# Edge sums of a graph layer: products as the stationary operand, one-hots of 64 nodes as the moving one

## The chip, the core and the metric

The kernel runs on one core of a Trainium2 chip. The metric is the device time of one execution in microseconds. Before the change three runs took 1311.8, 1334.03 and 1337.46 us, a median of 1334.03 us. TensorE is called PE, its weight loads PEld, VectorE DVE, ScalarE ACT, GpSimd POOL, and the queue of SyncE SP.

## The reference, cut to what matters

A graph layer on 3125 nodes and 50000 edges (sorted by destination) is followed by a mixture of experts. The graph layer, with constants left out:

```python
h0, h1 = x0 @ W_lin1_0 * z, einsum('nuc,uv->nvc', x1, W_lin1_1) * z      # node table h, 256 numbers a node
hid = silu(edge_length_embedded @ fc_w0)                                # 8 -> 64 an edge ("radial")
wA, wB, wC, wD = split(hid @ fc_w1)                                     # 4 x 64 an edge
xs0, xs1 = h0[edge_src], h1[edge_src]                                   # the gather
midA = wA * xs0 * sh0
midD = wD * einsum('euc,ec->eu', xs1, sh1) / sqrt(3)
midB = (wB * xs0)[:, :, None] * sh1[:, None, :]
midC = wC[:, :, None] * xs1 * sh0[:, None, :]
y = segment_sum(concat(midA, midD, midB, midC), edge_dst)               # the edge sums
out = s + (y @ W_lin2) * z                                              # then a residual and a layer norm
```

Everything is float32. A second layer norm, a router, a shared expert and eight routed experts (two a token) follow.

## The kernel before

The program is a chain of blocks, each with its own instruction streams for the five engines and a barrier at its end: `node_block`, `edge_block`, `update_block`, and the expert blocks. Nothing schedules the work: the order on each engine is the order in the text, and semaphores that count steps tie the engines together.

`node_block` (from line 134) normalises 25 tiles of 128 nodes and writes the table `h_tab` to memory. POOL clears `y_sb` (L262) and splits the edge lengths `ele` into a rounded high part and a remainder (L265, L267), which SP writes out as `ele_split`; it splits the two radial weight matrices too (L270 to L275). The high and low parts stand in a reduced type (F32R): a product of such operands takes one pass of PE per column, and two terms restore the precision.

`edge_block` (from line 448) works in T = 98 steps of 512 edges, four groups (C = 4) of 128 edges each. One more loop, over rounds r, repeats all steps when the destinations of some step span more nodes than the window; here one round is enough (392 gathers are 98 x 4), and since the widest step spans 37 nodes, a window of 64 nodes needs one round as well. In each step:

- SP loads the edge lengths of the step (L518); PE multiplies them with `w0` (`hidden`, L720, one matmul of 512 columns); ACT applies the silu (L566).
- DVE rounds the result (`high`, L616) and takes the remainder (`low`, L621); PE multiplies with `w1hi` and `w1lo` (`radial`, L728 and L729, eight matmuls of 256 columns, contraction over 128 rows).
- POOL copies the step's source numbers and factors sh to small tiles (L543, L547) and issues four gathers of 128 rows (L552) into one of two buffers `rows`.
- DVE compares the destinations with 0 to 127 (`one_hot`, L607, 512 elements a partition); ACT scales each one-hot with the four sh of its edge (`scale_hot`, L576, 16 instructions of 128 columns).
- DVE forms eight products of 64 a group (`products`, L634 and L636, one pair a group).
- PE sums over edges (`segment`): the scaled one-hots [128 edges x 128 nodes] are stationary, the products move. Each group is one matmul of 256 columns (L740) and three of 128 (L743), in plain float32.
- DVE adds the result, 128 nodes by 512, to `y_sb` in two halves of 64 partitions (`add_y`, L651).

PE runs in each turn `hidden(t+2)`, `radial(t+1)`, `segment(t)`; DVE runs `add_y(t-1)`, `high(t+2)`, `one_hot(t+2)`, `low(t+2)`, `products(t+1)`. In the trace one plain float32 matmul is two weight loads and two matmul records, one F32R matmul is one of each.

`update_block` (from line 764) takes 25 tiles: POOL copies 128 nodes of sums (L879), PE transposes them (`turn`, L1057, four matmuls), ACT copies the result (L983), PE multiplies with W_lin2 (`mix`, L1067, four float32 matmuls with 64 moving columns). Then come residual, norm, transposes and router scores (L1078, L1086 with 8 stationary columns, L1098).

## Time and profile before

| | us |
|---|---|
| median of 3 runs | 1334.03 |
| the profiled execution: its span | 1334.0 |
| node block | 0 to 65.5 |
| edge block, from the barrier to the first edge sum | 65.5 to 78.4 |
| edge block, first edge sum to the last | 78.4 to 682.2 |
| end of the edge block, update block | 682.2 to 779 |
| experts | 779 to 1334.0 |

The profiled execution's own time is the span of 1334.0 us; it is also the median run, so nothing lies between the two. Start times in the rows are microseconds from the start of the span. In rows of a timeline, instructions that are alike and follow each other are merged (x8), and the duration runs from the start of the first to the end of the last; a matmul's end is modelled, so paces are read from starts. An engine's idle time before a row stands in brackets, with what ended it.

### The profile page before, as it was taken

The page shows a single profiled execution, that of the slowest core. Times are in us where ns is not written, and L with a number is a line of the kernel's source. Part 1 is how long each engine was busy: PE and PEld are TensorE (multiplying, and loading weights), DVE is VectorE, ACT ScalarE, POOL GpSimd, SP SyncE. Part 2 cuts the span into 40 slices and gives each one's busy share as a digit, 9 for nine tenths or more (in the row PEclk, how much of TensorE's full clock was granted, in tenths as well). Part 3 has the DMA queues.
Part 4 walks back from the last instruction along what each step waited for, and adds up shares of the span by engine and source line. Part 5 has one row for each costly group of instructions (what it writes and reads, how often), then busy time and mean ns, then how long its engine had stood idle before and what let it go on. Part 6 is the DMA issues. An engine that isn't in the chain of part 4 may idle for free. (4 is left out here: it accounts for less than half of the span.)

```text
span 1334.0 us, 32063 instructions
## 1 busy us (share of the span) xinstructions
PE 1217.9 (91%) x8631; PEld 1120.6 (84%) x8632; DVE 1029.3 (77%) x2584; ACT 826.6 (62%) x2362; POOL 720.3 (54%) x823
## 2 busy tenths in 40 slices
PE   2789999999999999999989899998998997989995
PEld 2578888888888888888887679998998997989995
DVE  7589999999999999999856866444765674666663
ACT  2688888888888888888834674453442443343431
POOL 7178888788887888878731104651242232233332
PEclk9989999999999999999975979999999998999998
DMA  6443444344344444434543474764324334332232
GB/s 241 155 131 111 120 117 119 111 119 120 111 122 120 115 116 118 121 110 118 171 126 116 163 259 131 251 216 140 99 44 103 78 62 99 95 95 46 46 49 28
DMA packets 107219, 160.47 MB, mean 120 GB/s; under 512 B 16414, under 2 KB 82750, under 8 KB 106656
## 3 DMA queue, kind: packets, MB, share of 16 engines
q1 hardware_dynamic: 73680, 90.86, 21.4%
q0 software_dynamic: 29568, 65.62, 20.6%
q10 hardware_dynamic: 3920, 3.41, 0.8%
q8 instruction: 19, 0.31, 0.1%
q14 instruction: 32, 0.26, 0.1%
HBM read 110.99 MB, written 48.85 MB: 120 GB/s over the span
## 5 line engine op out<-in xcount | busy, mean ns | idle before, releaser
L576 ACT ACTIVATE hots<-hot,sh_st 128x128 f32<-128x128 f32 x1568 | 467.9, 390 | 3.8 <-PE psY L743 3.3
L552 POOL DMA_INDIRECT rows<-h_tab,src_st x392 | 404.9, 1033 | 117.2 <-issue 116.9
L743 PEld LDWEIGHTS psY<-prod,hots 128*128 128x128 f32 x2352 | 324.6, 192 | 20.4
L743 PE MATMUL psY<-prod,hots 128*128 128x128 f32 x2352 | 326.1, 275 | 0.0
L1739 POOL DMA_INDIRECT out_rows<-q_ob,q_index x58 | 125.5, 2163 | 294.4 <-DVE q_ob L1837 193.3
L740 PE MATMUL psY<-prod,hots 128*128 128x256 f32 x784 | 234.4, 381 | 0.6 <-DVE prod L636 0.6
L636 DVE TENSOR_TENSOR prod<-psW,rows 128x384 f32<-128x384 f32 x392 | 213.8, 545 | 0.0
L1763 ACT ACTIVATE q_hf<-q_psA,q_b 128x256 f32<-128x256 f32 x232 | 109.7, 473 | 111.7 <-PE q_psA L1293 109.0
L1300 PE MATMUL q_psB<-x_whi,q_hhi 128*128 128x256 f32 x464 | 138.7, 299 | 24.5 <-DVE q_hlo L1815 24.5
L651 DVE TENSOR_TENSOR y_sb<-y_sb,psY 64x512 f32 x196 | 133.4, 681 | 10.2 <-issue 5.7
L1293 PE MATMUL q_psA<-q_xhi,x_whi 128*128 128x256 f32 x464 | 133.2, 287 | 4.0 <-DVE q_xlo L1804 2.8
L1300 PE MATMUL q_psB<-x_wlo,q_hhi 128*128 128x256 f32 x464 | 133.7, 288 | 0.0
L1300 PE MATMUL q_psB<-x_whi,q_hlo 128*128 128x256 f32 x464 | 133.7, 288 | 0.0
L1293 PE MATMUL q_psA<-q_xlo,x_whi 128*128 128x256 f32 x464 | 131.5, 283 | 0.0
L1293 PE MATMUL q_psA<-q_xhi,x_wlo 128*128 128x256 f32 x464 | 131.5, 283 | 0.0
L728 PE MATMUL psW<-w1hi,cols_hi 128*128 128x256 f32 x392 | 108.2, 309 | 16.2 <-DVE cols_hi L621 6.5
L740 PEld LDWEIGHTS psY<-prod,hots 128*128 128x128 f32 x784 | 119.4, 191 | 0.8 <-DVE prod L636 0.8
L634 DVE TENSOR_TENSOR prod<-psW,rows 128x128 f32<-128x128 f32 x392 | 110.5, 282 | 5.4 <-DMA rows<-h_tab,src_st 1.8
L1300 PEld LDWEIGHTS q_psB<-x_whi,q_hhi 128*128 128x128 f32 x464 | 90.6, 195 | 28.0 <-issue 27.0
L566 ACT ACTIVATE hid<-psE 128x512 f32<-128x512 f32 x98 | 58.7, 598 | 89.2 <-PE psE L720 87.6
L728 PEld LDWEIGHTS psW<-w1hi,cols_hi 128*128 128x128 f32 x392 | 75.0, 191 | 45.8 <-issue 45.1
L729 PE MATMUL psW<-w1lo,cols_hi 128*128 128x256 f32 x392 | 98.0, 283 | 0.0
(213 smaller groups left out, 2509.6 us busy)
## 6 DMA issues: line engine op xcount, KB each, us to landing
x_raw<-in_w SPq DMA_DIRECT2D x18, 1024.0 KB, 8.0
slots_d<-blank SPq DMA_DIRECT2D x49, 258.0 KB
x_slot_tile<-slots_d SPq DMA_DIRECT2D x30, 258.0 KB, 2.8
s_row<-xn_d SPq DMA_DIRECT2D x50, 128.0 KB, 3.1
cols_lo<-ele_split SPq DMA_DIRECT2D x196, 32.0 KB
rows<-h_tab,src_st POOLq DMA_INDIRECT x392, 2.8
x_sb<-in_x SPq DMA_DIRECT2D x5, 640.0 KB, 5.8
h_tab<-x_sb ACTq DMA_DIRECT2D x5, 640.0 KB, 3.3
```

What stands on the lines that cost most here:

```text
L552: pool.indirect_dma_start(out=rows[p][:, c, :, :].rearrange("p a u -> p (a u)"), out_offset=None, in_=h_tab, in_offset=bass.IndirectOffset ...
L576: ins = nc.scalar.activation(hots[p][:, 4 * c + k, :], hot[p][:, c, :], ACT.Copy, scale=sh_st[p][:, 4 * c + k:4 * c + k + 1])
L634: nc.vector.tensor_tensor(slots[:, 0::7, :], w[:, 0:2, :], rows[p][:, c, 0:1, :].to_broadcast([P, 2, MUL]), ALU.mult)
L636: nc.vector.tensor_tensor(slots[:, 1:7, :].rearrange("p (b k) u -> p b k u", b=2), w[:, 2:4, :].unsqueeze(2).to_broadcast([P, 2, 3, MUL]), ...
L651: ins = nc.vector.tensor_tensor(acc, acc, psY[p][lo:lo + HALF, :], ALU.add)
L728: nc.tensor.matmul(o, hidT[p][:, P * c:P * c + P], w1hi[:], start=True, stop=False)
L740: ins = nc.tensor.matmul(y[:, 1::2, :], hots[p][:, 4 * c, :], a[:, 4:8, :], start=(c == 0), stop=(c == C - 1), skip_group_check=True)
L743: ins = nc.tensor.matmul(y[:, 2 * k::6 - 2 * k, :][:, 0:2, :], hots[p][:, 4 * c + k + 1, :], a[:, 0::k + 1, :][:, 0:2, :], start=False, st ...
L1293: ins = nc.tensor.matmul(ps, w1_part(w, k, f), x(k), start=(n == 0), stop=(n == len(terms) - 1))
L1300: ins = nc.tensor.matmul(ps, h, w2_part(w, f), start=(f == 0 and n == 0), stop=(f == FC - 1 and n == 2))
L1739: pool.indirect_dma_start(out=out, out_offset=bass.IndirectOffsetOnAxis(ap=index[m][:], axis=0), in_=ob[m][:], in_offset=None, compute_op= ...
L1763: nc.scalar.activation(hf[f][:], psA[f % 4][:, 0:TOK], ACT.Gelu, bias=b1_st[:, f:f + 1]).then_inc(gelu_done, 1)
```

## The change

- `segment` is transposed. The products are stationary, two blocks of 64 at a time (128 columns), and the scaled one-hots of a window of SPAN = 64 nodes move. There are five matmuls a group: two with the sh0 one-hot, on products (0,1) and (2,3), then one for each of the three sh1 one-hots, on products (4,5), (5,6) and (7,8). `products` writes nine blocks of 64 instead of eight, in four instructions a step instead of eight. The sums stand transposed in `yT` [128, 5, 3264], and `add_y` adds one tile of 128 by 320.
- The radial network runs in plain float32: `hidden` has a contraction of 16 rows and 256 columns (the two halves of the step stand beside each other in the block-diagonal `w0`), and `radial` has four matmuls of 64 rows and 256 columns, in the order of groups 0, 2, 1, 3; groups 0 and 1 use rows 0 to 63, groups 2 and 3 rows 64 to 127. `high`, `low`, `ele_split` and all splitting on POOL go.
- Silu, `one_hot` and `scale_hot` work on 256, 256 and 64 elements instead of 512, 512 and 128.
- POOL's copies go. The gathers are unrolled over 98 steps with a ring of seven buffers (four of them in memory borrowed from `wlo0`), one semaphore a buffer; SP loads sh for each step.
- In `update_block` the transposes and both copies go; `mix` is five float32 matmuls of 128 moving columns on a zero-padded `w2`, which ten small loads fill.

```diff
+SPAN = 64
+REG = 5
+NCOL = NPAD + SPAN
...
-            y_sb = gkeep("y_sb", [P, NT + 1, 8, MUL])
+            yT = gkeep("yT", [P, REG, NCOL])
...
-                residue = ekeep("residue", [P, T, C])
...
+                w0 = ekeep("w0", [2 * NB, P])
+                fc_w = ekeep("fc_w", [P, 4, MUL])
...
-            sp.dma_start(e_raw, ele_t.rearrange("b e -> (b e)").rearrange("(p w) -> p w", p=P)).then_inc(e_in, 16)
-            for dst, src in ((src_sb, v["src_t"]), (dst_ti, v["dst_t"]), (sh_sb, v["sh_t"])):
+            for dst, src in ((src_sb, v["src_t"]), (dst_ti, v["dst_t"])):
                 sp.dma_start(dst[:].rearrange("p t c -> p (t c)"), src).then_inc(tab_in, 16)
+            for n, column in enumerate((1, 0, 3, 2)):
+                sp.dma_start(fc_w[:, n, :], v["fc1"][:, MUL * column:MUL * (column + 1)]).then_inc(fc_in, 16)
             sp.wait_ge(fczero, 1)
             sp.wait_ge(pool_step, 2)
             for half in range(2):
-                sp.dma_start(w0raw[32 * half:32 * half + 2 * NB, :], v["fc0"]).then_inc(fc_in, 16)
-            sp.dma_start(w1raw[:], v["fc1"]).then_inc(fc_in, 16)
+                sp.dma_start(w0[NB * half:NB * (half + 1), MUL * half:MUL * (half + 1)], v["fc0"][0:NB, 0:MUL]
+                             ).then_inc(fc_in, 16)
...
-            flat = ele_split.rearrange("r e -> (r e)").rearrange("(h p w) -> h p w", h=2, p=P)
-            sp.wait_ge(e_split_hi, 1)
-            sp.dma_start(flat[0], e_hi.bitcast(F32)).then_inc(e_out, 16)
...
-            link(pool.memset(y_sb[:], 0.0))
...
+            link(pool.memset(yT[:], 0.0))
...
+    PART = STEP // 2
+    RING = 7
+    USES = T // RING
+    TURN = 2 * RING
+    assert T % TURN == 0
...
-        rows = [sb(f"rows{i}", [P, C, 4, MUL]) for i in range(2)]
-        prod = [sb(f"prod{i}", [P, C, 8 * MUL]) for i in range(2)]
-        hot = [sb(f"hot{i}", [P, C, P]) for i in range(2)]
-        hots = [sb(f"hots{i}", [P, 4 * C, P]) for i in range(2)]
+        hid = [sb(f"hid{i}", [P, PART]) for i in range(2)]
+        LENT = WW // (C * FEAT)
+        rows = [v["wlo0"][:, C * FEAT * i:C * FEAT * (i + 1)].bitcast(F32).rearrange("p (c a u) -> p c a u", c=C, a=4)
+                for i in range(LENT)]
+        rows += [sb(f"rows{i}", [P, C, 4, MUL])[:] for i in range(RING - LENT)]
+        prod = [sb(f"prod{i}", [P, C, 9, MUL]) for i in range(2)]
+        hot = [sb(f"hot{i}", [P, C, SPAN]) for i in range(2)]
+        hots = [sb(f"hots{i}", [P, C, 4, SPAN]) for i in range(2)]
...
-                            sp.dma_start(e_st[p][32 * half:32 * half + 2 * NB, :].bitcast(F32),
-                                         ele_split[:, at(first_edge, STEP)]).then_inc(e_in[p], 16)
+                            sp.dma_start(e_st[p][NB * half:NB * (half + 1), :],
+                                         ele_t[:, at(first_edge + PART * half, PART)]).then_inc(e_in[p], 16)
+                        first_sh = sp.snap(t * (4 * C))
+                        sp.wait_ge(hots_done, r * T + t + 1)
+                        sp.dma_start(sh_st[p][:], sh_t[:, at(first_sh, 4 * C)]).then_inc(sh_in[p], 16)
...
             with pool.Fori(0, R) as r:
-                with pool.Fori(0, T // 2) as k:
...
+                for t in range(T):
+                    pool.wait_ge(prod_done, (r * T + t) * 2 + 2)
+                    pool.sem_inc(gather_turn, 1)
+                    for c in range(C):
+                        pool.indirect_dma_start(
+                            out=rows[t % RING][:, c, :, :].rearrange("p a u -> p (a u)"), out_offset=None, in_=h_tab,
+                            in_offset=bass.IndirectOffsetOnAxis(ap=src_sb[:, t, c:c + 1], axis=0),
+                        ).then_inc(row_in[t % RING], 16)
...
-                act.wait_ge(low_done, r * T + j + 1)
-                nc.scalar.activation(hid[p][:], psE[:], ACT.Silu, scale=1.0 / float(np.sqrt(NB))).then_inc(silu_done, 1)
-            def scale_hot(r, j, p):
-                act.wait_ge(sh_staged, r * T + j + 1)
+                act.wait_ge(w_done, r * T + j + 1)
+                nc.scalar.activation(hid[p][:], psE[p][:, 0:PART], ACT.Silu,
+                                     scale=1.0 / float(np.sqrt(NB))).then_inc(silu_done, 1)
+            def scale_hot(r, k, j, p):
+                act.wait_ge(sh_in[p], 16 * (r * (T // 2) + k + 1))
                 act.wait_ge(hot_done, r * T + j + 1)
                 act.wait_ge(seg_done, r * T + j + 1)
                 for c in range(C):
-                    for k in range(4):
-                        ins = nc.scalar.activation(hots[p][:, 4 * c + k, :], hot[p][:, c, :], ACT.Copy,
-                                                   scale=sh_st[p][:, 4 * c + k:4 * c + k + 1])
+                    for n in range(4):
+                        ins = nc.scalar.activation(hots[p][:, c, n, :], hot[p][:, c, :], ACT.Copy,
+                                                   scale=sh_st[p][:, 4 * c + n:4 * c + n + 1])
...
-                nc.vector.tensor_tensor(hot[p][:], iota_row[:].unsqueeze(1).to_broadcast([P, C, P]),
-                                        key[:, at(j), :].rearrange("p o c -> p (o c)").unsqueeze(2).to_broadcast([P, C, P]),
+                nc.vector.tensor_tensor(hot[p][:], iota_row[:, 0:SPAN].unsqueeze(1).to_broadcast([P, C, SPAN]),
+                                        key[:, at(j), :].rearrange("p o c -> p (o c)").unsqueeze(2).to_broadcast([P, C, SPAN]),
                                         ALU.is_equal).then_inc(hot_done, 1)
...
-            def high(r, j, p):
...
+            def products(r, turn, j, p, ring):
                 dve.wait_ge(w_done, r * T + j + 1 + 2)
                 dve.wait_ge(seg_done, r * T + j + 1)
-                for c in range(C):
...
+                dve.wait_ge(row_in[ring], 16 * C * (r * USES + turn + 1))
+                w, x, out_p = psW[p], rows[ring], prod[p]
+                nc.vector.tensor_tensor(out_p[:, :, 1:4, :], w[:, :, 2:3, :].to_broadcast([P, C, 3, MUL]),
+                                        x[:, :, 1:4, :], ALU.mult)
+                nc.vector.tensor_tensor(out_p[:, :, 0, :], w[:, :, 0, :], x[:, :, 0, :], ALU.mult).then_inc(prod_done, 1)
+                nc.vector.tensor_tensor(out_p[:, :, 4::2, :], w[:, :, 3:4, :].to_broadcast([P, C, 3, MUL]),
+                                        x[:, :, 1:4, :], ALU.mult)
+                nc.vector.tensor_tensor(out_p[:, :, 5::2, :], w[:, :, 1:2, :].to_broadcast([P, C, 2, MUL]),
+                                        x[:, :, 0:1, :].to_broadcast([P, C, 2, MUL]), ALU.mult).then_inc(prod_done, 1)
             def add_y(r, j, p):
-                low_tile = dve.value_load(low_row[0:1, at(j)], min_val=0, max_val=NT)
-                high_tile = dve.value_load(high_row[0:1, at(j)], min_val=0, max_val=NT)
+                low = dve.value_load(low_row[0:1, at(j)], min_val=0, max_val=NPAD)
                 dve.wait_ge(seg_done, r * T + j + 1 + 2)
                 dve.wait_ge(y_done, r * T + j + 2)
-                for lo, tile in ((0, low_tile), (HALF, high_tile)):
-                    acc = y_sb[lo:lo + HALF, at(tile), :, :].rearrange("p o a u -> p (o a u)")
-                    ins = nc.vector.tensor_tensor(acc, acc, psY[p][lo:lo + HALF, :], ALU.add)
-                ins.then_inc(y_done, 1)
+                acc = yT[:, :, at(low, SPAN)]
+                nc.vector.tensor_tensor(acc, acc, psY[p][:, 0:REG * SPAN].rearrange("p (g n) -> p g n", g=REG), ALU.add
+                                        ).then_inc(y_done, 1)
...
+                def turn_of(r, k, q, last=False):
+                    j = k * TURN + 2 + q
+                    add_y(r, j - 2, q % 2)
+                    if not last:
+                        one_hot(r, j + 1, (q + 1) % 2)
+                    products(r, k * 2 + (2 + q) // RING, j, q % 2, (2 + q) % RING)
+                with dve.Fori(0, T // TURN - 1) as k:
+                    for q in range(TURN):
+                        turn_of(r, k, q)
...
-                nc.tensor.matmul(psE[:], w0[:], e_st[p], start=True, stop=True).then_inc(hid_done, 1)
+                nc.tensor.matmul(psE[p][:, 0:PART], w0[:], e_st[p][:], start=True, stop=True
+                                 ).then_inc(hid_done, 1)
             def radial(r, j, p):
-                pe.wait_ge(low_done, r * T + j + 1 + 2)
-                pe.wait_ge(prod_done, (r * T + j) * C + C)
-                for c in range(C):
-                    o = psW[p][c // 2][:, 256 * (c % 2):256 * (c % 2) + 256]
-                    nc.tensor.matmul(o, hidT[p][:, P * c:P * c + P], w1hi[:], start=True, stop=False)
-                    ins = nc.tensor.matmul(o, hidT[p][:, P * c:P * c + P], w1lo[:], start=False, stop=True)
+                pe.wait_ge(silu_done, r * T + j + 1 + 2)
+                pe.wait_ge(prod_done, (r * T + j) * 2 + 2 * RING - 2)
+                for c in (0, 2, 1, 3):
+                    part = slice(MUL * (c // 2), MUL * (c // 2) + MUL)
+                    ins = nc.tensor.matmul(psW[p][:, c, :, :],
+                                           hid[p][part, P * (c % 2):P * (c % 2) + P],
+                                           fc_w[part, :, :], start=True, stop=True)
                 ins.then_inc(w_done, 1)
             def segment(r, j, p):
                 pe.wait_ge(hots_done, r * T + j + 1 + 2)
                 pe.wait_ge(y_done, r * T + j + 1)
-                y = psY[p][:, :].rearrange("p (a u) -> p a u", u=MUL)
+                y = psY[p][:, 0:REG * SPAN].rearrange("p (g n) -> p g n", g=REG)
+                pe.wait_ge(prod_done, (r * T + j) * 2 + 1 + 2 * RING)
                 for c in range(C):
-                    pe.wait_ge(prod_done, (r * T + j) * C + c + 1 + 2 * C)
-                    a = prod[p][:, c, :].rearrange("p (a u) -> p a u", u=MUL)
-                    ins = nc.tensor.matmul(y[:, 1::2, :], hots[p][:, 4 * c, :], a[:, 4:8, :], start=(c == 0),
-                                           stop=(c == C - 1), skip_group_check=True)
-                    for k in range(3):
-                        ins = nc.tensor.matmul(y[:, 2 * k::6 - 2 * k, :][:, 0:2, :], hots[p][:, 4 * c + k + 1, :],
-                                               a[:, 0::k + 1, :][:, 0:2, :], start=False, stop=(c == C - 1),
+                    for g in range(2):
+                        nc.tensor.matmul(y[:, g, :], prod[p][:, c, 2 * g:2 * g + 2, :].rearrange("p a u -> p (a u)"),
+                                         hots[p][:, c, 0, :], start=(c == 0 and g == 0), stop=(c == C - 1),
+                                         skip_group_check=True)
+                pe.wait_ge(prod_done, (r * T + j) * 2 + 2 + 2 * RING)
+                for c in range(C):
+                    for n, first in enumerate((4, 5, 7)):
+                        ins = nc.tensor.matmul(y[:, 2 + n, :],
+                                               prod[p][:, c, first:first + 2, :].rearrange("p a u -> p (a u)"),
+                                               hots[p][:, c, n + 1, :], start=False, stop=(c == C - 1),
...
+            top, bottom = slice(0, MUL), slice(MUL, P)
+            w_a, w_d = v["w_20"][0:MUL, :], v["w_20"][MUL:2 * MUL, :]
+            w_b, w_c = v["w_21"][0:MUL, :], v["w_21"][MUL:2 * MUL, :]
+            sp.wait_ge(wzero, 1)
+            for part, g, n, block_w in ((top, 0, 0, w_a), (bottom, 0, 1, w_c), (top, 1, 0, w_c), (bottom, 1, 1, w_c),
+                                        (top, 2, 0, w_d), (bottom, 2, 1, w_b), (top, 3, 1, w_b), (bottom, 3, 0, w_d),
+                                        (top, 4, 1, w_b), (bottom, 4, 0, w_d)):
+                sp.dma_start(w2[part, g, n, :], block_w).then_inc(w_in, 16)
             sp.dma_start(wr[:], v["w_r"].rearrange("(k p) e -> p k e", p=P)).then_inc(w_in, 16)
...
-            with pool.Fori(0, NG) as g:
...
+            pool.memset(w2[:], 0.0).then_inc(wzero, 1)
         @block.vector
...
-            def turn(g, q, j):
+            def mix(g, q, j):
                 t, i = g * GROUP + j, (q + j) % 2
-                pe.wait_ge(staged, t + 1)
...
                 pe.wait_ge(gnn_done, t + 1)
-                for c in range(4):
-                    o = MUL * (c + 1) if c < 3 else 0
-                    ins = nc.tensor.matmul(psO[i][:, o:o + MUL], yT[:, i, P * c:P * c + P], w2[:, c, :],
-                                           start=True, stop=True)
+                o = psO[i][:, 0:FEAT].rearrange("p (c u) -> p c u", u=MUL)
+                for g_ in range(REG):
+                    cols = (o[:, 0:2, :], o[:, 2:4, :], o[:, 0:2, :], o[:, 0::2, :], o[:, 0::3, :])[g_]
+                    ins = nc.tensor.matmul(cols, yT[:, g_, P * t:P * t + P], w2[:, g_, :, :], start=(g_ == 0),
+                                           stop=(g_ == REG - 1), skip_group_check=True)
...
```

## Rows read from the trace of the kernel before

**Rows 1.** Windows by stage: length; busy PE, PEld, DVE, ACT, POOL; PE clock; DMA.
```profile
78.40:682.20 603.80, 588.46 (x4001) 527.63 (x3999) 583.03 (x1260) 510.15 (x1648) 479.46 (x578) 1.00 0.43 118
682.20:779.00 96.80, 81.85 (x475) 64.46 (x475) 61.28 (x188) 46.57 (x116) 16.00 (x25) 0.71 0.46 158
```

**Rows 2.** Timeline of DVE, one step: start, duration, engine, line, operation, tiles, shapes, count.
```profile
307.05 1.37 DVE L651 TENSOR_TENSOR y_sb<-y_sb,psY 64x512 f32 x2
...
310.54 0.29 DVE L634 TENSOR_TENSOR prod<-psW,rows 128x128 f32<-128x128 f32 x1
310.75 0.55 DVE L636 TENSOR_TENSOR prod<-psW,rows 128x384 f32<-128x384 f32 x1
311.21 0.28 DVE L634 TENSOR_TENSOR prod<-psW,rows 128x128 f32<-128x128 f32 x1
...
313.20 0.67 DVE L651 TENSOR_TENSOR y_sb<-y_sb,psY 64x512 f32 x1
```

**Rows 3.** Timeline of PE, the same stretch.
```profile
303.67 0.28 PE L743 MATMUL psY<-prod,hots 128*128 128x128 f32 x1
303.87 0.50 PE L720 MATMUL psE<-cols_lo,w 64*128 64x512 f32 x1
304.49 0.38 PE L728 MATMUL psW<-w1hi,cols_hi 128*128 128x256 f32 x1
...
305.53 0.59 PE L740 MATMUL psY<-prod,hots 128*128 128x256 f32 x2
305.96 0.83 PE L743 MATMUL psY<-prod,hots 128*128 128x128 f32 x6
306.63 0.60 PE L740 MATMUL psY<-prod,hots 128*128 128x256 f32 x2
```

**Rows 4.** The page's list of costliest groups: busy, mean ns, idle before.
```profile
L743 PEld LDWEIGHTS psY<-prod,hots 128*128 128x128 f32 x2352 | 324.6, 192 | 20.4
```

**Rows 5.** Timeline of PE's weight loads in the update block, at two clocks.
```profile
760.86 0.97 PEld L1067 LDWEIGHTS u_psO<-u_w,u_yT 128*128 128x128 f32 x8
...
696.04 3.11 PEld L1067 LDWEIGHTS u_psO<-u_w,u_yT 128*128 128x128 f32 x14
```

**Rows 6.** Timeline of PE in the update block, around a matmul with 8 stationary columns.
```profile
757.27 0.39 PE L1078 MATMUL u_psX<-ident,u_xn 128*128 128x128 f32 x2
757.59 0.60 PE L1086 MATMUL u_psX<-u_xT,u_wr 128*8 128x128 f32 x4
758.13 0.66 PE L1057 MATMUL u_psY<-ident,u_ys 128*128 128x128 f32 x4
```

**Rows 7.** Timeline of POOL in the edge block, two gathers of a step.
```profile
305.50 0.95 POOL L552 DMA_INDIRECT rows<-h_tab,src_st  x1 [0.31 <-issue]
306.75 0.94 POOL L552 DMA_INDIRECT rows<-h_tab,src_st  x1 [0.30 <-issue]
```

**Rows 8.** Timeline of ACT in the edge block, one step.
```profile
304.98 4.78 ACT L576 ACTIVATE hots<-hot,sh_st 128x128 f32<-128x128 f32 x16
```

**Rows 9.** Timeline of POOL and DVE in the node block.
```profile
3.85 11.19 POOL L262 MEMSET y_sb<- 128x13312 f32 x1
...
25.52 6.90 POOL L267 TENSOR_TENSOR x_wlo<-x_raw,x_whi 128x3136 fp32r<-128x3136 f32 x1
...
9.21 6.05 DVE L304 TENSOR_SCALAR xn<-x_sb,mv,rstd 128x192 f32<-128x192 f32 x1
...
25.69 6.78 DVE L302 TENSOR_SCALAR xn<-x_sb,mv,rstd 128x64 f32 x1
```

**Rows 10.** Windows in the update block: columns as in the first group.
```profile
685.70:730.10 44.40, 40.06 (x183) 34.33 (x182) 23.85 (x74) 15.32 (x35) 10.18 (x16) 0.50 0.42 137
730.10:767.70 37.60, 32.11 (x254) 25.25 (x253) 31.03 (x100) 24.39 (x64) 4.45 (x7) 1.00 0.52 183
```

**Rows 11.** Timeline of PE and SP at the start of the update block.
```profile
690.50 1.06 PE L1057 MATMUL u_psY<-ident,u_ys 128*128 128x128 f32 x4
...
685.36 0.59 SPq L831 DMA_DIRECT2D u_w<-in_w  x1
```

267 lines of the change are left out of this document (67 added, 200 removed).

## The prediction

> **What bounds the kernel now.** I read the windows by stage first. The edge sums take 603.8 us for 98 steps, 6.16 us a step, at the full clock (2.4 GHz); in them PE is busy 588, DVE 583, ACT 510 and POOL 479 us [rows 1]. Four engines are nearly full, so busy time does not say who leads. The timelines of one step do. DVE goes from one `add_y` to the next in 313.20 - 307.05 = 6.15 us without an idle note [rows 2]: it sets the pace. PE has slack in one place. Its last sum starts at 303.67, `hidden` at 303.87, `radial` at 304.49 although `hidden` is one matmul of 512 columns, and the next sum at 305.53. A group of sums repeats after 306.63 - 305.53 = 1.10 us, four make 4.40 [rows 3]. So PE's own work is 4.40 + 1.04 (`radial`) + about 0.3 (`hidden`) = 5.75 us, only 0.4 below DVE. Whatever is taken from DVE, the step can shrink by 0.4 us, if PE's work stays as it is. That is the question: what does the change do to PE?
>
> **PE's edge sums.** Before, a group has one float32 matmul of 256 moving columns and three of 128, 16 in a step; after, it has five of 64, 20 in a step. Columns are halved (2560 to 1280), but each matmul also loads 128 stationary columns twice. The present 128-column sums come every 0.11 us a record: six records last 0.83, of which the last one's own 0.28 comes off, over five paces [rows 3]. A load takes 192 ns by itself [rows 4]. Would 64 columns go faster? The update block holds exactly this form, `mix`: eight loads span 0.97 us, less 0.19 for the last, over seven paces: 0.112 us a record, the same as at 128 columns; at the low clock fourteen loads span 3.11 us, 0.21 to 0.22 a record [rows 5]. So at 64 columns the load sets the pace, and halving the columns buys nothing. New sums: 40 records x 0.112 = **4.48 us** against 4.40.
>
> **PE's radial network.** Eight reduced matmuls of 256 columns cost 1.04 us. After, four float32 ones of 256 columns are eight records. One such record takes as long as L740's, two of which go from 305.53 to 305.96: 0.215 us [rows 3]. In line: 8 x 0.215 = 1.72 us. But each uses only 64 rows, and the order 0, 2, 1, 3 alternates between the lower and upper rows. If neighbours on different rows run beside each other, while the two records of one matmul don't, five slots of 0.215 remain: **1.08 us**. No row of this trace has two such neighbours, so the ends are 0.86 (all in pairs) and 1.72; I take 1.08, because the pieces share neither rows nor, as 0 and 2 lie in different banks, output. `hidden` becomes two records of 256 columns: **0.43 us**.
>
> The Trainium skill ("TensorEngine Tiling (Array Packing)", Key Properties) says that tiles of the array run loads and matmuls in parallel; by it alone `radial` would be 0.86 to 1.08. No run here shows it yet.
>
> **Changes of shape.** Where the occupied part of the array changes, PE pauses. L1078 starts two records at 757.27, which end their pace at 757.49; L1086, with 8 columns, starts at 757.59, 0.10 later; its four records would be through at 758.03, and L1057 starts at 758.13, again 0.10 [rows 6]. The load that could not be taken ahead is exposed on top, up to 0.11 (one pace). I take 0.15 a change, from 0.10 to 0.20. Before, there are two a step (`hidden` has 64 rows), inside PE's slack. After, rows go 16, 64, 128: three, **0.45 us**, if 16 and 64 rows count as different.
>
> The same section of the page says that changing the mode drains TensorE; it gives no price, and rows 6 agree with a pause.
>
> PE's step after: 4.48 + 1.08 + 0.43 + 0.45 = **6.44 us**, all in one line since PE would be the only full engine.
>
> **The other engines.** DVE: a product of 128 elements starts 0.21 before the next, one of 384 0.46 [rows 2], that is 0.98 ns an element and 0.085 an instruction. New products: 2304 elements in four, 2.60; sum of 320, 0.40; one-hot of 256, 0.34; together 3.3 us, with `high` and `low` gone. ACT: sixteen scaled one-hots of 128 columns last 4.78 [rows 8]; at 64 they can't last longer, and the silu halves, so at most about 5.2. POOL: a gather comes every 1.25 us [rows 7], four make 5.0, and its copies go; unrolling doesn't touch that. All lie under 6.44, with one to three us to spare, so their savings, and the nine blocks in place of eight, are worth nothing in time; if PE were faster than 5.2, ACT and POOL would be next. SP's new load of sh waits for the one-hots of two steps before, and the next step's edge lengths queue behind it. `hidden` wants them more than a step later, so I price this at nothing; the cover is that step of over 6 us.
>
> **Outside the step.** Node block: POOL's clearing grows from 13312 to 16320 elements, 11.2 to 13.7 us, and DVE, which stands behind it (6.05 us), loses 2.5; the split that held DVE for 6.78 goes [rows 9]: -4 us. Start of the edge block: earlier by its short chain on DVE, later by float32 at the low clock, 0. End: one sum less, -1. Update block: a tile loses four transposes (at the low clock four paces of 0.21, 0.85; the four last 1.06 with their tail [rows 11]) and gains two records of 128 columns, 0.43. That is -0.42 on some 13 tiles at the low clock and -0.2 on 12 at the full one [rows 10], -8 in all; the first `mix` waits for five more loads of weights, 0.6 us each [rows 11], and their clearing, +4. So -4. Sum outside: **-9 us**, give or take 7.
>
> **The sum.** 98 x (6.44 - 6.16) = +27; with -9, +18: 1334 + 18 = **1352 us**. The profiled execution is the median itself. Its fastest sister took 1311.8, so a run can differ by 20 us; the update block spends 44 us at half clock with PE busy 40 of them [rows 10], which shows that the clock can be late. Such a difference is within 2%, about what a measurement of this kernel can tell from no change.
>
> **The rivals.**
> - *No overlap in `radial` (slower).* The four matmuls go one after the other: 1.72 in place of 1.08. PE 7.08 us, 98 x 0.92 = +90, -9: **1415 us**. For it: in every row shown, matmuls start in line. Against it: none of these has neighbours on different rows. It decides from a step of 6.53 us on (+2%), that is when `radial` costs more than 1.17 us. 0.32.
> - *PE is lighter than I count (faster).* All pairs overlap (0.86) and two changes of shape at 0.10 remain: 4.48 + 0.86 + 0.43 + 0.20 = 5.97. 98 x -0.19 - 9 = -28: **1306 us**. Loads for free rows could be taken ahead; but the sums alone, 4.48, rest on a measured pace. 0.15.
> - *The clock falls.* The new sums move 64 columns in the time of 128, and in the update block PE was busy 40 of 44 us at the low clock [rows 10], with such matmuls in it. At 0.213 a record the step doubles, near **1970 us**. Against it: the same work stays at the full clock in the next 38 us, and `radial` fills a quarter of the step. 0.03.
> - My forecast has 0.50; its own range is 6.30 to 6.60 us a step, 1335 to 1370.
>
> The change may not do what it says if the window of 64 nodes didn't hold a step, and all steps ran twice; the widest step spans 37, so I give this nothing.
>
> **Chances and range.** Faster by over 2% (under 1307): half of the light case and a little for what I have not thought of, 0.14. Slower by over 2% (over 1361): the rival without overlap, the clock, and the upper fifth of the forecast, 0.32 + 0.03 + 0.10 = 0.45. Within: 0.41. The range from 1300 to 1422 leaves out the clock, the lower part of the light case and the upper of the slow one.
>
> **What would show it.** In a step after: the sums' records 0.112 apart (40 of them); `radial` starts in pairs of a few ns and five slots, or eight starts 0.215 apart; pauses of 0.10 to 0.20 at three places; DVE idle some 3 us a step; gathers still 1.25 apart, with waits for the ring. I am wrong if the sums' records are closer than 0.11, if PE waits in the step for ACT, POOL or a transfer, or if the half clock stands in the edge block's row.

## The result, and the profile after

The changed kernel takes **1873 us** (median of 4 runs, 1869.95 to 1874.78) where the kernel before takes 1332 (median of 4, 1311.8 to 1337.46): 1.418 times as long, interval 1.405 to 1.430. The times of experiments below leave out runs in the slow state unless a range is given. Forecast were 1352 us and a range to 1422. What came is the rival "the clock falls", which had a chance of 0.03 and a price of 1970 us.

Windows of the changed kernel, columns as in [rows 1]: edge block from its first hidden product, update block, experts.

```profile
64.10:1209.50 1145.40, 1144.93 (x4814) 989.81 (x4814) 345.45 (x579) 412.32 (x1650) 371.83 (x391) 0.50 0.22 60
1209.50:1320.00 110.50, 87.06 (x542) 71.75 (x542) 64.58 (x204) 41.78 (x118) 0.88 (x3) 0.77 0.44 150
1320.00:1867.00 547.00, 500.73 (x3962) 493.93 (x3961) 328.34 (x977) 225.94 (x485) 195.53 (x183) 0.96 0.41 105
```

The third last column is the news: the granted clock is 0.50 (1.2 GHz) in the whole edge block, where [rows 1] had 1.00, with PE busy all the time. The line of the granted clock in the page, 40 equal slices (a digit is tenths of 2.4 GHz, 5 is the half clock), shows it at a glance:

```profile
PEclk9655555555555555555555555569899999999998
```

The clock did not fall from this work. In both kernels it was down already in the wait between the node block and the edge block: at 0.50 from 64.52 us on in the kernel before, from 58.20 on in the changed one. Before, it was back at 78.17, 8 us after the first hidden product (70.20) and just ahead of the first edge sum. After, it did not come back until 1242.6, in the update block. Two windows of the kernel before:

```profile
64.60:78.10 13.50, 5.67 (x17) 4.00 (x18) 9.86 (x25) 7.52 (x21) 8.44 (x13) 0.50 0.44 116
78.20:665.20 587.00, 571.67 (x3891) 511.77 (x3890) 569.47 (x1229) 501.55 (x1619) 473.33 (x571) 1.00 0.43 120
```

PE's timeline of one step of the changed kernel:

```profile
401.61 1.22 PE L644 MATMUL psE<-e_st,w 16*128 16x256 f32 x2
402.76 2.08 PE L653 MATMUL psW<-fc_w,hid 64*128 64x256 f32 x8
404.77 3.67 PE L666 MATMUL psY<-hots,prod 128*128 128x64 f32 x16
408.24 5.33 PE L672 MATMUL psY<-hots,prod 128*128 128x64 f32 x24
413.49 0.79 PE L644 MATMUL psE<-e_st,w 16*128 16x256 f32 x1
```

From hidden to hidden it is 11.88 us. The first sum starts at 404.77, the last of the 40 at 413.14: 0.213 to 0.215 a record, as the low clock's row of [rows 5] has it. From the first hidden record to that of the last step there are 97 steps: 1133.5 us against 592.5, that is +541 of the 534 by which the spans differ; all else together is -7 (-9 forecast).

Rows of the page's list of costliest groups (busy, mean ns, idle before and its cause) show that DVE waits for PE, and POOL for buffers that DVE frees:

```profile
L672 PEld LDWEIGHTS psY<-hots,prod 128*128 128x128 f32 x2352 | 513.5, 333 | 0.0
L594 DVE TENSOR_TENSOR yT<-yT,psY 128x320 f32 x98 | 47.9, 489 | 597.5 <-PE psY L672 597.5
L511 POOL DMA_INDIRECT x_wlo<-h_tab,src_sb x224 | 213.5, 953 | 398.7 <-DVE prod L584 340.6
```

The load rows stand beside [rows 4]: 333 ns in place of 192.

### The profile page after: what moved, and what is told of

The parts are those of the page before. It is cut to its first block and busy times, and to the rows that moved or that the text cites. A ratio compares the mean times of both kernels' runs of the same rounds, so it can differ in the third digit from the quotient of the medians.

```text
span 1867.9 us, 31686 instructions
## 1 busy us (share of the span) xinstructions
PE 1765.6 (95%) x9463; PEld 1580.2 (85%) x9464; DVE 777.1 (42%) x1887; ACT 711.5 (38%) x2337; POOL 586.3 (31%) x594
## 5 line engine op out<-in xcount | busy, mean ns | idle before, releaser
L672 PE MATMUL psY<-hots,prod 128*128 128x64 f32 x2352 | 522.1, 421 | 0.0
L672 PEld LDWEIGHTS psY<-hots,prod 128*128 128x128 f32 x2352 | 513.5, 333 | 0.0
L666 PEld LDWEIGHTS psY<-hots,prod 128*128 128x128 f32 x1568 | 341.6, 330 | 63.2 <-issue 62.5
L536 ACT ACTIVATE hots<-hot,sh_st 128x64 f32<-128x64 f32 x1568 | 385.0, 334 | 6.6 <-PE psY L672 6.4
L666 PE MATMUL psY<-hots,prod 128*128 128x64 f32 x1568 | 360.0, 424 | 0.0
L511 POOL DMA_INDIRECT x_wlo<-h_tab,src_sb x224 | 213.5, 953 | 398.7 <-DVE prod L584 340.6
L594 DVE TENSOR_TENSOR yT<-yT,psY 128x320 f32 x98 | 47.9, 489 | 597.5 <-PE psY L672 597.5
L511 POOL DMA_INDIRECT rows<-h_tab,src_sb x168 | 159.9, 952 | 307.1 <-DVE prod L584 257.1
L653 PE MATMUL psW<-fc_w,hid 64*128 64x256 f32 x784 | 203.8, 671 | 0.0
L653 PEld LDWEIGHTS psW<-fc_w,hid 64*128 64x128 f32 x784 | 116.1, 320 | 80.2 <-issue 63.0
L644 PE MATMUL psE<-e_st,w 16*128 16x256 f32 x196 | 119.3, 710 | 9.1 <-DMA e_st<-in_ele_t 9.0
L579 DVE TENSOR_TENSOR prod<-psW,x_wlo 128x768 f32<-128x768 f32 x56 | 53.6, 958 | 128.5 <-PE psW L653 120.7
```

What stands on the lines that cost most here:

```text
L511: pool.indirect_dma_start(out=rows[t % RING][:, c, :, :].rearrange("p a u -> p (a u)"), out_offset=None, in_=h_tab, in_offset=bass.Indirec ...
L536: ins = nc.scalar.activation(hots[p][:, c, n, :], hot[p][:, c, :], ACT.Copy, scale=sh_st[p][:, 4 * c + n:4 * c + n + 1])
L579: nc.vector.tensor_tensor(out_p[:, :, 1:4, :], w[:, :, 2:3, :].to_broadcast([P, C, 3, MUL]), x[:, :, 1:4, :], ALU.mult)
L594: nc.vector.tensor_tensor(acc, acc, psY[p][:, 0:REG * SPAN].rearrange("p (g n) -> p g n", g=REG), ALU.add).then_inc(y_done, 1)
L644: nc.tensor.matmul(psE[p][:, 0:PART], w0[:], e_st[p][:], start=True, stop=True).then_inc(hid_done, 1)
L653: ins = nc.tensor.matmul(psW[p][:, c, :, :], hid[p][part, P * (c % 2):P * (c % 2) + P], fc_w[part, :, :], start=True, stop=True)
```

## The experiments

**Theories.** A: the narrow sums, 64 moving columns under a load of 128 stationary ones, keep the clock at 0.50. B: the block merely lacks a stretch of dense work at its start that lifts the clock, and would keep it. C: the float32 radial product on 64 rows and the changes of shape keep it down.

The experiments ran on three chips (numbers 3, 10 and 12; that of the first comparison is not known). In their rounds the kernel before takes 1404 to 1412 us. All kernels whose PE runs at the full clock show holes there: PE and SP get their next instruction only after some 0.70 us or a multiple. So times are compared with the kernel before beside them, and paces are read from steps without a hole.

**e1: a warm-up written out.**

```diff
+                for i in range(60):
+                    nc.tensor.matmul(psY[0][:, :], some[:, 0:P], some[:, P:P + 512], start=True, stop=True)
                 with pe.Fori(0, T // 2 - 1) as k:
```

> The changed kernel with 60 extra matmuls of 512 moving columns (bf16, results thrown away) on TensorE between its first radial product and its loop of steps. Nothing in the loop is changed. Theory A (the new sums cannot hold the full clock: a record of 64 moving columns takes as long as its load of 128, so the array idles half of its time): the granted clock rises to 1.00 in the stretch and falls back to 0.50 early in the loop; the step is 11.88 us again and the time 1873 + about 15 to 20, so 1885 to 1895 us. Theory B (the block only never got the stretch of dense work that lifts the clock, and would keep it once lifted): the loop stays at 1.00, a step is 6.0 to 6.4 us and the time 1310 to 1360 us. Theory C (the float32 radial product on 64 rows and the three changes of shape pull the clock down, not the sums): as theory A, so this run does not tell A from C.

1947 us (one run); inconclusive. The clock rose at 72.3 us, but the last of the 60 came 0.7 to 2.8 us apart, and it fell at 86.0, ahead of the first step at 108. The steps take 11.88 us again, so the half clock does not belong to the first comparison alone.

**e7: the warm-up as a loop of four matmuls, 30 turns.**

> The changed kernel (64 columns a sum) with 120 matmuls of 512 columns ahead of the loop of steps again, now as a short loop of four, since 60 written out came 0.7 to 2.8 us apart at their end and let the clock fall ahead of the first step. Theory A: the clock is at 1.00 when the first steps begin, some of them take about 6.3 us, and it falls to 0.50 within a few steps and stays there: 1873 us and 30 more. Theory B: it stays at 1.00 to the end of the block, about 1370 us.

1936 us (one run). The clock is at 1.00 from 109.00 to 153.40, then falls and stays down for the block. The first 13.3 us of that stretch are the end of the warm-up; the steps begin at 122.36, so they ran at the full clock for 31 us: four in 6.30 us each, and most of a fifth. Windows of this kernel, and a step at the full clock (same columns as above):

```profile
109.00:153.40 44.40, 42.96 (x287) 30.99 (x285) 14.21 (x24) 17.83 (x72) 15.51 (x16) 1.00 0.23 62
153.40:1230.00 1076.60, 1076.60 (x4532) 932.30 (x4533) 325.29 (x547) 386.01 (x1547) 328.58 (x344) 0.50 0.21 57
```

```profile
128.66 0.69 PE L644 MATMUL psE<-e_st,w 16*128 16x256 f32 x2
129.28 1.14 PE L653 MATMUL psW<-fc_w,hid 64*128 64x256 f32 x8
130.34 2.00 PE L666 MATMUL psY<-hots,prod 128*128 128x64 f32 x16
132.18 2.84 PE L672 MATMUL psY<-hots,prod 128*128 128x64 f32 x24
134.95 0.48 PE L644 MATMUL psE<-e_st,w 16*128 16x256 f32 x1
```

134.95 - 128.66 = 6.30 us (by the unrounded starts): 11.88 is the same work at the other clock. But ahead of the fall four records came late, 0.55 to 0.76 us behind the ones before them, between 148.7 and 152.3, so this run does not say that the clock falls without them. Against B it shows that what was lost never came back, in 1076 us without a hole; e6, below, on the same chip, loses the clock in holes too and gets it back each time.

**e2, e6: 96 moving columns, 32 of them thrown away.**

```diff
-                                         hots[p][:, c, 0, :], ...
+                                         wide[:, SPAN * 4 * c:SPAN * 4 * c + WIDE], ...      # WIDE = 96
...
-                                               hots[p][:, c, n + 1, :], ...
+                                               wide[:, SPAN * (4 * c + n + 1):SPAN * (4 * c + n + 1) + WIDE], ...
```

> The changed kernel, but each sum moves 96 columns in place of 64: 32 columns that follow in the one-hots go along, and their results are thrown away. Loads, their number, DVE's and ACT's work stay. Theory A: with 96 columns under each load the clock holds at 1.00 through the edge block. Then a record still goes at its load's pace of 0.11 us, the step is 4.48 + 0.86 (radial in pairs) + 0.43 + 0.3 to 0.4 for the changes of shape = about 6.05 us, and the time 1334 - 98 x 0.1 - 9 = about 1315 us (1300 to 1340). Theory B: nothing lifts the clock, 0.50 throughout, a record of 96 columns at 0.213 still: 1873 us. Theory C: the same, 1873 us.

> The kernel that moves 96 columns again, for a time without the holes. Its undisturbed steps at the full clock took 6.324 us against 6.157 in the kernel before and 11.88 in the changed one. Theory A: full clock throughout the block; 1334 + 98 x 0.167 - 9 = about 1341 us where the kernel before takes 1334. Theories B and C, by which 96 columns change nothing, are already out by the first run. If holes come again: a time above the kernel before by 5 to 11%.

e2 takes 1535 and 1557 us beside 1411, and e6 takes 1549 beside 1408 (ratio 1.104, interval 1.098 to 1.110). The changed kernel took 1873 in the first comparison and, with e7's warm-up of some 50 us, 1936 on e6's chip, with fewer columns moved. The window is the block of e6, the timeline a step in it:

```profile
64.20:841.00 776.80, 695.54 (x4763) 597.76 (x4763) 339.10 (x573) 404.52 (x1633) 374.44 (x391) 0.88 0.32 86
```

```profile
185.95 0.69 PE L648 MATMUL psE<-e_st,w 16*128 16x256 f32 x2
186.58 1.13 PE L657 MATMUL psW<-fc_w,hid 64*128 64x256 f32 x8
187.64 2.02 PE L671 MATMUL psY<-hots,prod 128*128 128x96 f32 x16
189.50 2.84 PE L677 MATMUL psY<-hots,prod 128*128 128x96 f32 x24
192.28 0.69 PE L648 MATMUL psE<-e_st,w 16*128 16x256 f32 x2
```

24 records of 64 or of 96 columns last 2.84 us: the load sets the pace, and the extra columns are free. The clock is at 1.00 throughout 71 of the 97 steps (61 of them take 6.32 us each, without a hole), and from 120 us on each stretch at 0.50 lasts only 3.4 to 6.8 us. The clock also rose while PE ran these sums without a hole, at 119.6, with the last late record at 110.7. With 64 columns on the same chip (e1, e7) it never ends in the block. So A holds, and B and C are out as the whole cause. Left open is whether 64 columns would lose a clock that nothing disturbs: ahead of every fall seen under such sums there are late records. What is left of 776.8 - 97 x 6.32 = 163 us is holes and the half clock behind them:

```profile
177.41 0.35 PE L671 MATMUL psY<-hots,prod 128*128 128x96 f32 x1 [0.33 <-issue]
178.10 0.24 PE L671 MATMUL psY<-hots,prod 128*128 128x96 f32 x1 [0.34 <-issue]
178.82 0.45 PE L671 MATMUL psY<-hots,prod 128*128 128x96 f32 x2 [0.47 <-issue]
180.23 1.96 PE L671 MATMUL psY<-hots,prod 128*128 128x96 f32 x12 [0.96 <-issue]
```

**e3: the kernel before with the new radial network alone** (hidden, radial, silu and their loads as after, high and low gone; sums, gathers and windows as before).

```diff
-                    nc.tensor.matmul(o, hidT[p][:, P * c:P * c + P], w1hi[:], start=True, stop=False)
-                    ins = nc.tensor.matmul(o, hidT[p][:, P * c:P * c + P], w1lo[:], start=False, stop=True)
+                    ins = nc.tensor.matmul(psW[p][:, c, :, :]..., hid[p][part, P * (c % 2):P * (c % 2) + P],
+                                           fc_w[part, :], start=True, stop=True)
```

> The kernel before with the float32 radial network alone: hidden as two halves of 256 edges, radial as four float32 matmuls on 64 rows in the order 0, 2, 1, 3, no splits, no high and low; sums, gathers, windows and update block as before. Theory A: the sums move 128 and 256 columns, so the clock holds at 1.00. TensorE's step is 4.40 + 0.86 + 0.43 + about 0.3 = 6.0 us against 6.15, the node block some 3 us shorter: 1305 to 1335 us. Theory C: the radial form keeps the clock at 0.50 and the step is about 11.7 us: 1860 us. Theory B: unclear, the lift at the start of the block could be missed as in the changed kernel (1860 us) or not.

1434 us in one run (1458 to 1484 in three others) beside 1411, the clock 0.95 over the block, steps without a hole 6.29. So C is out, and the new radial network is no gain by itself: PE's step is 6.29 where the kernel before has 5.96 on these chips (e9).

**e13: the kernel before with narrow sums.** Half of the products are left out of its sums.

```diff
-                    ins = nc.tensor.matmul(y[:, 1::2, :], hots[p][:, 4 * c, :], a[:, 4:8, :], ...
+                    for g in range(2):
+                        ins = nc.tensor.matmul(y[:, 1 + 2 * g:2 + 2 * g, :], hots[p][:, 4 * c, :], a[:, 4 + g:5 + g, :], ...
...
-                                               a[:, 0::k + 1, :][:, 0:2, :], ...
+                                               a[:, 0:1, :], ...
```

> The kernel before (one-hots stationary, products moving, reduced radial, its own hidden) with its sums made as narrow as the new ones: in each group five matmuls of 64 moving columns in place of one of 256 and three of 128, half of the products left out of the sums, so its output is not the reference's. 40 records x 0.112 = 4.48 us beside 4.40, so TensorE's own work stays about 5.8 us a step, near DVE's pace. Theory A (narrow sums under full loads are what the clock falls from, in whichever form): the clock is at 0.50 in most or all of the block, the step 2 x 4.27 + 8 x 0.213 + 0.5 = about 10.9 us and the time 1870 to 1890 us. Theory C, as the last that is left of it (it takes the float32 radial on 64 rows, the changes of shape and the narrow sums together): the clock stays at 1.00 but for the holes, the step 5.9 to 6.1 us, the time 1400 to 1420 us where the kernel before takes 1408.

1695 us (one run) beside 1410. Line of the granted clock, a window at either clock, and the whole block:

```profile
PEclk9755755575575557665757977798899999999998
```

```profile
192.80:353.20 160.40, 160.40 (x705) 152.19 (x705) 87.24 (x196) 77.10 (x249) 63.51 (x90) 0.50 0.23 67
353.20:377.10 23.90, 22.03 (x181) 20.90 (x180) 19.05 (x45) 17.65 (x58) 12.63 (x18) 1.00 0.37 96
69.60:980.30 910.70, 894.64 (x4666) 846.78 (x4666) 557.17 (x1246) 503.78 (x1627) 410.90 (x579) 0.62 0.28 78
```

PE's sums just before the fall at 192.8:

```profile
188.50 0.72 PE L744 MATMUL psY<-prod,hots 128*128 128x64 f32 x5
190.16 0.22 PE L744 MATMUL psY<-prod,hots 128*128 128x64 f32 x1 [0.94 <-issue]
190.21 0.30 PE L741 MATMUL psY<-prod,hots 128*128 128x64 f32 x1
191.62 0.52 PE L741 MATMUL psY<-prod,hots 128*128 128x64 f32 x3 [1.10 <-issue]
```

Narrow sums hold the clock down in the old form too, with the reduced radial on 128 rows beside them: A, with nothing of C in it. Each of the seven falls within the block comes 1.1 to 1.3 us behind such late records, so here too the full clock ends behind a hole. The difference is what follows: six of the seven stretches at 0.50 behind them last 38 to 160 us, where those of e9, the same kernel with wide sums, last 3.4 to 6.8. A step at 0.50 takes 11.15 us (10.9 expected). The time came out lower than expected because the clock comes back eight times in the block. In the new form it never did in 98 steps; what the old one adds are eight reduced matmuls of 256 columns a step, but that this is the difference was not tested.

**e4, e5, e14: the new sums in column halves.**

```diff
-                        nc.tensor.matmul(y[:, g, :], prod[p][:, c, 2 * g:2 * g + 2, :]..., hots[p][:, c, 0, :], ...
+                        for h in range(2):
+                            nc.tensor.matmul(y[MUL * h:MUL * h + MUL, g, :], prod[p][:, c, 2 * g + h, :], hots[p][:, c, 0, :], ...
```

> The changed kernel with each sum cut in two: 64 stationary columns (one product) for the lower half of the output's partitions, 64 for the upper half, 64 columns moving in each. 80 records in place of 40. Theory A says that the clock follows how much of the time columns move. If a load of 64 columns takes half as long and the two halves run beside each other as the radial pairs do, 40 pairs take 40 x 0.056 = 2.2 us at the full clock, columns move all the time and the clock holds; TensorE's step is 3.9 us and the gathers, 4 x 1.25 = 5.0 us, set it: about 1215 to 1240 us. If the halves run beside each other but a load of 64 takes as long as one of 128, the sums stay at 40 x 0.112 or, at the half clock, 40 x 0.213: 1870 us. If they run one after the other at half the load: 4.5 us again, at a clock that theory A lets be full: 1315 us. Theories B and C: clock at 0.50, so 4.4 + 3.3 = 7.8 us a step at best, about 1490 us.

> The kernel with the sums cut in column halves again. In its first run TensorE was short of instructions in stretches of each turn of its loop (matmuls without a wait 0.7 to 2.8 us apart), and the kernel before took 1411 in place of 1334 us beside it. In the stretches between, at the full clock, a step was 4.2 us. Theory A (columns now move in both halves nearly all the time, so the clock holds): where the instructions come in time, the step is set by the gathers, 5.0 us, and the time is 1215 to 1250 us. Rival D (80 matmul records a step in place of 40 are more instructions than the queue brings, so the holes belong to this kernel): holes again and about 1600 us or more, even where the kernel before takes 1334.

> The kernel with column halves a third time, for a run without holes in the stream of instructions. Without holes: gathers set the step at 5.0 us, 1215 to 1250 us where the kernel before takes 1334. With holes as before: 1650 to 1690 us. Anything between would say that the holes differ from chip to chip more than the kernels do.

1662, 1667 and 1672 us beside 1408 to 1411 (ratio 1.18, 1.19, 1.19). The sums of a step of e14 with a hole, and one of its last steps, when the gathers are done:

```profile
144.45 1.26 PE L667 MATMUL psY<-hots,prod 128*64 128x64 f32 x31
146.12 0.22 PE L667 MATMUL psY<-hots,prod 128*64 128x64 f32 x1 [0.42 <-issue]
146.16 0.32 PE L674 MATMUL psY<-hots,prod 128*64 128x64 f32 x2
146.92 0.32 PE L674 MATMUL psY<-hots,prod 128*64 128x64 f32 x2 [0.43 <-issue]
148.31 2.50 PE L674 MATMUL psY<-hots,prod 128*64 128x64 f32 x44 [1.08 <-issue]
...
972.24 0.69 PE L644 MATMUL psE<-e_st,w 16*128 16x256 f32 x2 [0.88 <-DMA e_st<-in_ele_t]
972.86 1.14 PE L653 MATMUL psW<-fc_w,hid 64*128 64x256 f32 x8
973.92 1.15 PE L667 MATMUL psY<-hots,prod 128*64 128x64 f32 x32
974.90 1.57 PE L674 MATMUL psY<-hots,prod 128*64 128x64 f32 x48
976.40 0.48 PE L644 MATMUL psE<-e_st,w 16*128 16x256 f32 x1
```

The halves run beside each other and load in half the time: 80 records and the way to the next hidden take 976.40 - 973.92 = 2.48 us, a step of 4.17 in place of 6.30. But a hole of some 6 us comes in nearly every second step, the clock is at 0.71 over the block (it comes back after each hole, so 64 moving columns do not keep it down under a load of 64), and the 1215 to 1250 us never came. The missing gain is in the holes and the half clock behind them (D was right that this kernel has most of them; the kernel before has some too, e9). No run without holes shows the gain.

**e8: radial in the order 0, 1, 2, 3** (on the kernel with 96 columns).

> The kernel that moves 96 columns with the four radial matmuls in the order 0, 1, 2, 3, so that neighbours stand on the same rows but for 1 and 2. If only neighbours on different rows run beside each other: 6 slots of 0.215 in place of 4, or 8 if a pair must start together; the undisturbed step at the full clock grows from 6.324 to 6.75 or to 7.18 us. If the order doesn't matter: 6.32.

1549 us (one run); the undisturbed step is 6.33, and radial's eight records still start as four pairs, 13 ns apart. The forecasts of six and of eight slots were wrong: PE pairs records across the order of the text.

**e12, e15: hidden on 64 rows** (`w0` and `e_st` as 64 rows, 48 of them zero; 96 columns).

> The kernel that moves 96 columns, with hidden on 64 rows (48 of them zeros) in place of 16, so that hidden and radial have the same shape and a step has two changes of shape in place of three. In its undisturbed steps at the full clock (6.324 us) the three changes cost about 0.18 each by the gaps: hidden's first record 0.205 behind the last sum in place of 0.112, its second 0.320 behind the first in place of 0.215, radial's first 0.304 behind, its second pair 0.313 behind. If the occupied rows are what counts: 6.324 - 0.19 = 6.13 us. If a change of row tile (hidden over both halves, radial on one) costs the same as before: 6.32 us.

> The kernel with 96 columns and hidden on 64 rows. Its undisturbed step is 6.125 us. Without holes: 1334 - 98 x 0.03 - 9 = about 1322 us where the kernel before takes 1334, within 2%. With holes as in its first run: 1540 to 1565 us beside 1408.

1558 us (one run), and 1563 beside 1410 (ratio 1.109). The step is 6.125 in place of 6.324: one change of shape costs 0.20 us. Radial's first record now starts 0.01 behind hidden's, but the ten records of the two still take six slots, so that pairing is not the gain. The time does not follow, for the holes.

**e9, e10, e11, e16, e17: where the holes come from.** e9 is the kernel before unchanged. e10 and e11 move SP's blank writes in the halves kernel and in the kernel before:

```diff
+                with sp.Fori(0, T // 8) as k:
+                    turn(k, 4, 0)          # two steps and four writes
+                with sp.Fori(0, 1) as k:
+                    turn(k + T // 8, 1, 0)
+                with sp.Fori(0, T // 2 - T // 8 - 1) as k:
+                    turn(k + (T // 8 + 1), 0, 0)
```

e16 (halves) and e17 (96 columns, hidden on 64 rows) write PE's loop out:

```diff
-                with pe.Fori(0, T // 2 - 1) as k:
-                    for p in range(2):
+                with pe.Fori(0, (T // 2 - 1) // 8) as k:
+                    for p in range(16):
```

> The kernel before, unchanged, with a profile. Beside the experiments it took 1408 to 1411 us in place of 1334. If the holes in TensorE's stream of instructions (matmuls without a wait some 0.70 us apart) come from where the kernels run, and not from the new forms of the sums: holes here as well, about 75 us of them and of the half clock that follows, and steps of 6.157 us between. If the kernel before has none, the 75 us lie elsewhere, and the holes belong to the kernels with more matmuls a step.

> The kernel with the sums in column halves, and SyncE's 49 writes of blank rows (258 KB each, one in two steps) issued four at a time in the first 24 steps, so that the other 74 steps have none. Theory E (instructions come late because their own transfers stand behind these writes): no holes in the later three quarters, the clock there at 1.00 and the steps at the 5.0 us of the gathers; 1411 - 60 = about 1350 us here, 1240 to 1280 where no holes are. Theory F (they stand behind the gathers, or the supply is slow by itself): holes go on in the later steps as before, and the time stays at 1640 to 1690 us.

> The kernel before with the same shift of the blank writes into its first 24 steps. Theory E: no holes in its later three quarters, 1340 to 1370 us beside 1408 for the unchanged one. Theory F: no difference, 1400 to 1420 us. If the unchanged kernel shows no holes at all: no difference either.

> The kernel with column halves, and TensorE's loop written out eight turns long (6 turns of 16 steps in place of 48 of 2). In the looped version a hole of about 6 us comes once in nearly every turn, mostly at matmul 40 to 60 of its second step. Theory G (the holes come from the return to the loop's head, for which instructions are brought again): holes once in 16 steps, the clock near 1.00, the step near the gathers' 5.0 us and the time 1300 to 1400 us, below the kernel before beside it. Theory H (the supply can't keep pace with a TensorE that never waits, loop or not): holes as often or more, 1650 us and above.

> The kernel with 96 columns and hidden on 64 rows, TensorE's loop written out in the same way. Theory G: holes in one step of 16, the clock near 1.00, steps of 6.125 us and about 1400 us beside 1410 for the kernel before (1335 to 1345 where no holes are). Theory H: 1560 us as looped, or more.

The measure is PE's idle time from 110 to 700 us that the profile puts down to issue, which means that PE waited for nothing that the profile shows:

| kernel | us of 590 |
|---|---|
| before and after, first comparison | 0 |
| e9, before (1404 us) | 18 |
| e3, before with the new radial network | 40 |
| e6, 96 columns | 46 |
| e17, 96 columns, loop written out | 47 |
| e10, halves, writes early | 155 |
| e16, halves, loop written out | 149 |
| e14, halves | 160 |

e9's steps without a hole take 5.96 us, less than the 6.15 of [rows 2]. That is PE's own step: in the first comparison, too, the kernel before makes eight steps in a row of 5.96, from 82.9 us on, with PE never idle, before DVE's pace of 6.16 takes over. e10: 1647 beside 1408, and from 320 us on, where there are no writes, PE still loses 98 of 380 us (e14: 106): E is out. e11: 1417 (one run), no gain. e16: 1658 beside 1412, e17: 1550, the holes as looped: G is out. That leaves a supply too slow for a PE that never waits. For it: the steps at 0.50 of e1, e7 and e13 show no hole, the kernel before, whose PE waits for DVE in most steps of the first comparison, loses least, and the halves kernel with its 90 records a step loses most. e3 fits: it has 42 records a step to 41 of the kernel before, and in these 590 us its PE waits 3 us for other engines, e9's 6. What the supply stands behind stays open, and why the first comparison showed no hole.

## Why the prediction was wrong

- **The clock: wrong, and this is the whole miss.** The sum took the step at 1.00, and the step that failed is the "against it" of the third rival: "the same work stays at the full clock in the next 38 us, and `radial` fills a quarter of the step". It was not the same work: of PE's 254 records in the 37.6 us of [rows 10] 104 are `mix` with its 64 moving columns, of the 50 of a new step 40 are such. And a clock that is up for a while says nothing of whether it comes back once it is down. e7 shows the new steps at 1.00 for 31 us and then 1076 us at 0.50; the changed kernel's block began at 0.50 and stayed there, 541 us more than before, while 96 columns in place of 64 brought the clock back after each fall (e2, e6). The half of [rows 10] that spoke for the rival, 44.4 us at 0.50 with PE busy for 40, was the one to believe. That the rival came true at a chance of 0.03 is no credit to the prediction. The Trainium skill, TensorE: Matmul & The Clock Gate (Part 1, What's actually happening), says that the gate follows how busy PE has recently been. By the profile's busy time that would have given 1.00 here: PE was busy for 1144.93 of 1145.40 us, at 0.50. The measurement decides: a PE that is busy in the profile can stay at the half clock.
- **The rival's price, 1970: too high by 97.** It doubled the step of 6.44; the real one goes from 6.30 to 11.88. That is 0.72 short of double: 0.40 because a sum's record goes from 0.112 to 0.213 and not to 0.224, and 0.3 because the pauses of changes of shape go from 0.53 to 0.79 only.
- **Edge sums, 4.48: right.** They take 0.112 a record at 1.00, 0.213 at 0.50; 64 and 96 columns alike.
- **PE's own step before, 5.75: 0.2 too small.** It is 5.96 (e9, and the eight steps named above), so PE had 0.2 us of slack below DVE and not 0.4. The forecast did not use it.
- **Radial, 1.08: the favourable end was true.** Eight records start as four pairs some 7 ns apart, in four slots: 0.86. So the second of the two records of a matmul pairs as well. The Trainium skill, TensorEngine Tiling (Array Packing), Key Properties, was right to say that tiles work in parallel, and e14 shows it for columns too (pairs 0.006 apart). The rival of 1415 us rested on the opposite and is refuted.
- **Changes of shape, 0.45: a little more.** At the full clock 6.30 - 4.48 - 0.86 - 0.43 = 0.53, and e12 measures one alone at 0.20, the upper end.
- **PE's step: 6.44 forecast, 6.30 at the full clock.** At that clock the change would have been 1334 + 98 x (6.30 - 6.157) - 7 = 1341 us (6.157 is the median step before), no difference that counts; worked out, not run.
- **Other engines: right.** DVE waits 597.5 us for the sums, 6.1 a step at the half clock; POOL waits for the ring; halving their work was worth nothing.
- **Outside the step, -9: right.** The first hidden product starts at 64.1 in place of 70.2; with the end it is -7, although the last two sums run at the low clock.

## What to carry to other kernels

Before narrowing the moving operand of a float32 matmul under a full load, ask what it does to the clock: where the load sets the pace, halving the columns gains nothing (0.112 us at 64, 96 and 128) and can keep the full clock away for a whole block (0.50 in place of 1.00, 11.88 in place of 6.30 us a step). A short stretch at the full clock is no evidence for such work. Look for what it does once the clock is down, as it was here at the start of the block in both kernels, and see that the rows are of the same mix of matmuls. If columns must be few, moving some useless ones is the cheap way out (1549 us); cutting the stationary side as well, so that two halves run side by side, has the shorter step (4.17) but took 1662 to 1672 here, with 160 of 590 us lost in holes.

## What the runs showed of the hardware

- Moving 32 useless columns more made the changed kernel faster: 1535 to 1557 us against 1873, in rounds where the kernel before took 6% longer.
- With PE busy throughout, the clock stayed at 0.50 for 1145 us under sums of 64 moving and 128 stationary columns. Under 96 moving columns (e6) the stretches at 0.50 lasted 3.4 to 6.8 us from 120 us on; in the old form with 64 (e13) six of seven lasted 38 to 160 us.
- Two column halves of 64 load and multiply beside each other at 0.058 us a pair at 1.00, half of what 128 stationary columns take (0.112).
- Records on different row halves pair even where the text puts two matmuls of the same half next to each other (e8).
- In the rounds of the experiments instructions reached PE and SP 0.70 us apart for several us at a time; in the halves kernel this took more than the new form gained (a step of 4.17 us without it, 9.5 with it: 920.80 us over 97).
